# A decoder block's expert routing: logits taken from eight extra columns of the output product of the linear attention, ahead of the row norm

## The reference

```python
x = x + cross_attention(ln(x), ctx_1024)         # 16 heads, 1024 keys per batch and a null key
x = x + gated_linear_attention(ln(x))            # 4 heads; ends in o.reshape(b, n, 512) @ Wo
x = x + ffn(ln(x))
# ffn, with t = ln(x), 8 experts, top 2, at most 40 rows an expert:
scores = softmax(t @ wg)                         # wg: 256 x 8
gates, idx = top_k(scores, 2); gates /= sum(gates)
# rows go to their slots, y = fc2(silu(fc1(row) + b1)) + b2 per expert
res = t + sum(gates * y)
out = layernorm(res) * ln_gamma + ln_beta
```

## Time and profile before

| what | value |
| --- | --- |
| three timed runs, median | 213.72 us (212.79, 213.72, 213.93) |
| profiled execution, span from first to last instruction | 211.1 us |
| median less span | 2.6 us |
| TensorE busy | 193.9 us, 92% of the span |
| VectorE, ScalarE, GpSimd busy | 145.0, 118.1 and 39.0 us |
| mean granted TensorE clock | 0.988 |
| routing: from the first DVE instruction behind `lw_psum` to the first gather on TensorE | 162.85 to 168.99 us |
| experts: first `up` to last `combine` | 170.13 to 206.6 us |

### The profile page before, as it was taken

The page is one execution under the profiler, slowest core; times in us unless marked ns, Lnnn a source line. Parts: engine busy times, 40 slices in busy tenths (PEclk is TensorE's granted clock), DMA queues, the critical chain, the costliest instruction groups (busy, mean ns, idle before and its releaser), DMA issues.

```text
span 211.1 us, 4137 instructions
## 1 busy us (share of the span) xinstructions
PE 193.9 (92%) x1627; PEld 147.4 (70%) x1629; DVE 145.0 (69%) x249; ACT 118.1 (56%) x221; POOL 39.0 (18%) x40
## 2 busy tenths in 40 slices
PE   6796579999999999999999999999988899999991
PEld 1693469999889988899888787956655344645560
DVE  3449798989799799999979869633873727224313
ACT  3187678987779777797878764005631123332300
POOL 4129301304022040120400800020501400000001
PEclk9799999999999999999999999999999999999998
DMA  5896649693302003020000399999999400000000
GB/s 171 278 390 188 168 138 313 227 302 114 99 3 99 3 0 102 0 53 0 2 3 0 120 381 312 342 380 378 378 378 377 146 0 0 3 0 0 3 0 28
DMA packets 22853, 31.02 MB, mean 147 GB/s; under 512 B 1953, under 2 KB 18866, under 8 KB 22834
## 3 DMA queue, kind: packets, MB, share of 16 engines
q1 hardware_dynamic: 22834, 30.76, 43.6%
HBM read 29.57 MB, written 0.13 MB: 141 GB/s over the span
## 4 chain that ended last, share of the span: by engine, by line
PE 58%; issue 21%; DVE 9%; ACT 3%; DMA 3%; POOL 2%; SPq 1%; POOLq 0%; DVEq 0%; ACTq 0%
PE ps L1022 38%; PE ps L1056 7%; DMA w_k_stage<-in_Wkv 3%; DVE keys L745 3%; PE ps L1096 2%; PE ps L1110 2%; PE ps L1210 1%; PE ps L1010 1%; DVE q_split L736 1%; PE ps L1083 1%; DVE ex_l L711 1%; PE ps L1194 1%; PE ps L1249 1%; DVE ex_sum L766 1%; POOL hT L545 1%
## 5 line engine op out<-in xcount | busy, mean ns | idle before, releaser
L745 DVE SCALAR_TENSOR_TENSOR keys<-ps,keys 64x512 f16<-64x512 f32 x64 | 44.1, 689 | 2.3 <-ACT keys L577 0.3
L1022 PE MATMUL ps<-ctxT_h,w_k_h 128*128 128x256 f32 x128 | 38.1, 298 | 2.4 <-DVE keys L745 2.1
L577 ACT ACTIVATE keys<-ps 64x512 f16<-64x512 f32 x64 | 37.9, 592 | 1.8
L1022 PE MATMUL ps<-ctxT_h,w_k_l 128*128 128x256 f32 x128 | 36.6, 286 | 0.0
L1022 PE MATMUL ps<-ctxT_l,w_k_h 128*128 128x256 f32 x128 | 36.5, 285 | 0.0
L711 DVE TENSOR_TENSOR ex_l<-ps,ex_h 128x512 fp32r<-128x512 f32 x32 | 22.0, 689 | 11.1 <-ACT ps L607 11.0
L606 ACT ACTIVATE ex_h<-ps 128x512 fp32r<-128x512 f32 x32 | 19.1, 596 | 15.6 <-PE ps L1056 15.5
L1022 PEld LDWEIGHTS ps<-ctxT_h,w_k_h 128*128 128x128 f32 x128 | 24.8, 194 | 3.8 <-issue 3.0
L1022 PE MATMUL ps<-ex_h,ctx_h 128*128 128x512 f32 x64 | 25.4, 397 | 0.0
L1022 PE MATMUL ps<-ex_l,ctx_h 128*128 128x512 f32 x64 | 25.1, 392 | 0.0
L1022 PE MATMUL ps<-ex_h,ctx_l 128*128 128x512 f32 x64 | 24.9, 389 | 0.0
(11 more groups left out here) (175 smaller groups left out, 262.7 us busy)
## 6 DMA issues: line engine op xcount, KB each, us to landing
w<-in_fc1T SPq DMA_DIRECT2D x8, 1024.0 KB, 12.2
w<-in_fc SPq DMA_DIRECT2D x8, 1024.0 KB, 12.0
stage_t<-in_ctxT SPq DMA_DIRECT2D x8, 256.0 KB, 3.4
stage_n<-in_ctx SPq DMA_DIRECT2D x8, 256.0 KB, 2.7
w_k_stage<-in_Wkv SPq DMA_DIRECT2D x4, 256.0 KB, 6.5
mixT<-in_Wq SPq DMA_DIRECT2D x2, 512.0 KB, 6.2
q_two<-q_split SPq DMA_DIRECT2D x8, 128.0 KB, 4.0
w_v<-in_Wkv SPq DMA_DIRECT2D x1, 1024.0 KB, 6.8
```

The source lines that it names most:

```text
L577: nc.scalar.activation(keys[rows, u % 2, PK * i:PK * (i + 1), r], full[rows].rearrange("p (j n) -> p j n", j=PK), ACT.Copy, scale=UNIT).th ...
L745: V.scalar_tensor_tensor(out=keys[other, u % 2, PK * i:PK * (i + 1), r], in0=ps[mine, K_BANK + kp % 2].rearrange("p (j n) -> p j n", j=PK) ...
L1022: last = MM(dst, lhs[i], rhs[j], start=start and m == 0, stop=stop and m == len(parts) - 1)
```

## The change

The logits no longer wait for the normalised rows. Eight columns are added to the output product of the linear attention: `w_lo` becomes 264 wide, and its last eight columns are Wo times the router's weights with each of their columns centred (`w_rc`); `x1` becomes 264 wide too, its last eight columns being the centred logits of the layer's input, `xn` times `w_route` times the row's standard deviation. Bank 4 thus holds rows and centred logits together, the latter short of the factor 1/std of the row, which is applied only in the exponential (`scale=stat[:, 2, 9:10]`).

- SP loads Wo a second time, transposed on the host (`w_loT`, 512 KB), behind `w_lo`.
- TensorE: a product with ones for the column sums (in place of two of ten fillers), the eight-column product of `xn` behind the keys, eight products of `w_loT` with `w_rc` between L1231 and L1235, 264 instead of 256 columns in L1240 and L1249. The transpose of `xn`, the logit product and the seven fillers around them go; the `xn` product into bank 4 moves behind the first `up`. Three and eight fillers stand where six, one and six stood.
- DVE: `w_rc` (one instruction), the eight columns of `x1` (one), then after `lw_psum` the top-two search comes first and the statistics after it; it writes only the centred rows `xc`; `x2` moves between the two one-hots.
- ACT: a copy of 32 columns into `w_lo`; the copy of `xnT` goes; ACT writes `xn_h` and `xn` from `xc`.
- POOL: makes `xn_l` (before: DVE) and clears only the unused slots of `hT`.
- `share` takes the place of `ex_sum`'s memory, `silu` is halved in place, to make room.

```diff
-        x1 = keep("x1", [P, D])
+        x1 = keep("x1", [P, D + E])
...
-        w_lo = keep("w_lo", [P, LH, D])
+        w_lo = keep("w_lo", [P, LH, D + E])
+        w_loT = keep("w_loT", [P, DC, LH * LDV])
+        w_rc = keep("w_rc", [P, DC, E])
...
-        share = alloc(attn_b, "share", [P, G, PG, P])
+        share = ex_sum[:].rearrange("p h b s -> p (h b s)").rearrange("p (g x j t) -> p g x j t", g=G, x=2, j=PG)[:, :, 0]
...
+        fin = alloc(moe, "fin", [P, 2, D])
+        xc = fin[:, 0]
...
-            sp.dma_start(w_lo[:], chunked("lWo")).then_inc(ld_lin, 16)
+            sp.dma_start(w_lo[:, :, 0:D], chunked("lWo")).then_inc(ld_lin, 16)
+            sp.dma_start(w_loT[:], chunked("lWoT")).then_inc(ld_lin, 16)
...
-                    nc.gpsimd.memset(hT[:], 0.0).then_inc(zero_ready, 1)
+                    pool.wait_ge(xn_ready, 3)
+                    low_part(xn_l[:], xn[:], xn_h[:]).then_inc(xn_split, 1)
+                    nc.gpsimd.memset(hT[:].rearrange("p n c e s -> p (n c e) s")[:, :, CAP:SLOTS], 0.0).then_inc(zero_ready, 1)
...
+            act.wait_ge(w_lr_psum, 1)
+            copy(w_lo[:, :, D:D + E], ps[:, 0, 0:LH * E].rearrange("p (h e) -> p h e", e=E), w_lr_ready)
...
-            act.wait_ge(xnT_psum, 3)
-            copy(xnT[:], ps[:, 0, 0:DC * P].rearrange("p (c t) -> p c t", c=DC), xnT_ready)
+            act.wait_ge(xc_ready, 1)
+            act.wait_ge(rstd_ready, 3)
+            nc.scalar.activation(xn_h[:], xc, ACT.Copy, scale=stat[:, 2, 9:10]).then_inc(xnh_ready, 1)
+            act.wait_ge(xnh_ready, 1)
+            nc.scalar.activation(xn[:], xc, ACT.Copy, scale=stat[:, 2, 9:10]).then_inc(xn_ready, 1)
             act.wait_ge(below_ready, 1)
-            nc.scalar.activation(top_exp[:], below[:], ACT.Exp, accum_out=gate_sum[:, 0:1]).then_inc(top_exp_ready, 1)
+            nc.scalar.activation(top_exp[:], below[:], ACT.Exp, scale=stat[:, 2, 9:10],
+                                 accum_out=gate_sum[:, 0:1]).then_inc(top_exp_ready, 1)
...
+            dve.wait_ge(colsum_psum, 1)
+            V.scalar_tensor_tensor(out=w_rc[:], in0=ps[:, 4, 0:E].unsqueeze(1).broadcast_to([P, DC, E]), scalar=-1.0 / D,
+                                   in1=w_route[:], op0=ALU.mult, op1=ALU.add).then_inc(w_rc_ready, 1)
...
+            dve.wait_ge(x1_logit_psum, 1)
+            V.tensor_scalar(x1[:, D:D + E], ps[:, 0, 0:E], stat[:, 1, 8:9], stat[:, 1, 9:10], ALU.mult,
+                            ALU.mult).then_inc(x1_ready, 1)
...
-            norm_stats(2, ps[:, 4, 0:D])
-            normalise(2, xn[:], ps[:, 4, 0:D]).then_inc(xn_ready, 1)
-            V.tensor_tensor(x2[:], ps[:, 4, 0:D], beta[:], ALU.add).then_inc(x2_ready, 1)
-            dve.wait_ge(xn_ready, 3)
-            link(V.tensor_copy(xn_h[:], xn[:]))
-            low_part(xn_l[:], xn[:], xn_h[:]).then_inc(xn_split, 1)
-            dve.wait_ge(rl_psum, 1)
-            logits = ps[:, 1, 0:E]
+            logits = ps[:, 4, D:D + E]
             link(V.max(top[:], logits))
             link(V.max_index(top_idx[:], top[:], logits))
             V.tensor_tensor(pick[:], iota8.unsqueeze(1).broadcast_to([P, 2, E]),
                             top_idx[:, 0:2].unsqueeze(2).broadcast_to([P, 2, E]), ALU.is_equal).then_inc(pick_ready, 1)
+            norm_stats(2, ps[:, 4, 0:D])
+            V.tensor_scalar(xc, ps[:, 4, 0:D], stat[:, 2, 6:7], None, ALU.subtract).then_inc(xc_ready, 1)
             V.tensor_scalar(below[:], top[:], top[:, 0:1], None, ALU.subtract).then_inc(below_ready, 1)
...
             one_hot(slice(0, P))
+            V.tensor_tensor(x2[:], ps[:, 4, 0:D], beta[:], ALU.add).then_inc(x2_ready, 1)
             one_hot(slice(P, E * SLOTS))
...
-            warm(10, 7)
+            pe.wait_ge(ld_lin, 16 * 9)
+            pe.wait_ge(ld_const, 16)
+            for c in range(DC):
+                last = MM(ps[:, 4, 0:E], ones, w_route[:, c], start=c == 0, stop=c == DC - 1)
+            last.then_inc(colsum_psum, 1)
+            warm(8, 7)
...
+            for c in range(DC):
+                last = MM(ps[:, 0, 0:E], xnT[:, c], w_route[:, c], start=c == 0, stop=c == DC - 1)
+            last.then_inc(x1_logit_psum, 1)
...
+            pe.wait_ge(w_rc_ready, 1)
+            pe.wait_ge(att_ready, 1)
+            for h in range(LH):
+                for c in range(DC):
+                    last = MM(ps[:, 0, h * E:(h + 1) * E], w_loT[:, c, h * LDV:(h + 1) * LDV], w_rc[:, c], start=c == 0,
+                              stop=c == DC - 1)
+            last.then_inc(w_lr_psum, 1)
...
-            MM(ps[:, 4, 0:D], eye, x1[:], start=True, stop=False)
-            warm(6, 0)
+            pe.wait_ge(x1_ready, 2)
+            MM(ps[:, 4, 0:D + E], eye, x1[:], start=True, stop=False)
+            warm(6, 1)
...
-                last = MM(ps[:, 4, 0:D], loT[:, h], w_lo[:, h], start=False, stop=h == LH - 1)
+                if h == 0:
+                    pe.wait_ge(w_lr_ready, 1)
+                last = MM(ps[:, 4, 0:D + E], loT[:, h], w_lo[:, h], start=False, stop=h == LH - 1)
             last.then_inc(lw_psum, 1)
-            warm(6, 7)
-            transpose_xn(2)
-            warm(2, 7)
-            pe.wait_ge(xnT_ready, 3)
-            for c in range(DC):
-                last = MM(ps[:, 1, 0:E], xnT[:, c], w_route[:, c], start=c == 0, stop=c == DC - 1)
-            last.then_inc(rl_psum, 1)
-            pe.wait_ge(x2_ready, 1)
-            MM(ps[:, 4, 0:D], eye, xn[:], start=True, stop=False)
-            warm(1, 7)
+            warm(3, 7)
             pe.wait_ge(triangle_ready, 2)
             pe.wait_ge(pick_ready, 1)
             MM(ps[:, 2, 0:2 * E], strict_b[:], pick[:].rearrange("p k e -> p (k e)"), start=True, stop=False,
                skip_group_check=True)
             MM(ps[:, 2, E:2 * E], ones_b[:], pick[:, 0], start=False, stop=True, skip_group_check=True).then_inc(loc_psum, 1)
-            warm(6, 7)
+            warm(8, 7)
...
             up(0)
+            pe.wait_ge(x2_ready, 1)
+            MM(ps[:, 4, 0:D], eye, xn[:], start=True, stop=False)
...
+    arrays["lWoT"] = v["L0_attn_Wo"].T```

TensorE behind the last half of the output gate's product. Before (`decay_p` is `loT`, `qx` under L1244 is the gated heads):

```order
L1231 MATMUL ps<-w_lg,xnT 128x512
L1235 MATMUL ps<-lv,att 128x128 x4
L1240 MATMUL ps<-x,const 128x256
L1010 MATMUL ps<-warmer 128x512 x6
L1244 MATMUL ps<-const,qx 128x128 x4
L1249 MATMUL ps<-w_lo,decay_p 128x256 x4
```

More of the change, by code:

```diff
@@ L650, in _ @@
             act.wait_ge(g_psum, 1)
-            nc.scalar.activation(silu[:, 0], ps[:, 5], ACT.Tanh, scale=0.5).then_inc(gtanh_ready, 1)
+            nc.scalar.activation(silu[:], ps[:, 5], ACT.Tanh, scale=0.5).then_inc(gtanh_ready, 1)
+            act.wait_ge(w_lr_psum, 1)
+            copy(w_lo[:, :, D:D + E], ps[:, 0, 0:LH * E].rearrange("p (h e) -> p h e", e=E), w_lr_ready)
             for h in range(LH):
@@ L1368 @@
     arrays["ctxT"] = arrays["ctx"].T
+    arrays["lWoT"] = v["L0_attn_Wo"].T
     arrays["Wgk2b"] = np.concatenate([v["L0_attn_Wgk2"], v["L0_attn_bgk2"][None, :]])
```

21 lines of the change are left out of this document (12 added, 9 removed).

## The result

| | before | after |
| --- | --- | --- |
| median of 19 runs each | 213.57 us | 212.28 us |
| lowest to highest run | 211.77 to 215.06 | 210.91 to 213.32 |
| ratio, with its 95% interval | | 0.9951 (0.9931 to 0.9971) |
| span of the profiled execution | 211.1 us | 211.2 us |

By the ratio the kernel is faster by 1.05 us (0.6 to 1.5); the two medians by themselves differ by 1.29, which lies in that interval. The forecast was 0.88 us less and 212.8 us, made against a median of 213.72.

What follows compares the result with a forecast made beforehand. TensorE was taken to bound from the first `up`, a serial routing path before it. -2.09 + 0.71 + 0.05 + 0.45 = -0.88 us, from 213.72 to 212.8 us; range 212.0 to 214.1.

Steps and rivals of the forecast that it cites:

- The bound: From the first `up` on TensorE bounds; bringing the first gather forward comes off the end, work added to TensorE goes on.
- Term 1: Routing path from T (first DVE instruction behind `lw_psum`) to the first gather's load: 6.14 us becomes 4.05, gain 2.09.
- I hold `below` until the power ends.: Routing on DVE: `below` waits for POOL's power on the shared memory port, until T+2.04; escaping would gain 0.13 us more.
- the rival of the longer rows' branch: Power, two ACT passes, POOL: passes up to half longer than 0.417 us, gather moves 0.43, result 213.3 us; chance 0.08.
- The collision, "T+4.05": One-hot's second half and POOL's `xn_l` meet on the shared port near T+3.0; gather at T+4.05 instead of undisturbed T+3.85.
- Term 2: Eight products of `w_loT` and `w_rc` before the values: 16 instructions at 0.11 us, 0.71 us lost.
- the rival that ended slower: The eight weight products do not pipeline, each fresh load shows: 214.1 or 215.2 us; chance 0.04.
- Term 3: Eight more columns in the output product (L1249): 0.05 us lost.
- Term 4: The `xn` product moved behind the first `up`, where TensorE has no gap: 0.45 us lost.
- T at 163.6: Expected profile sign: the first DVE instruction behind `lw_psum`, at 162.85 before, comes at 163.6 us.
- At nothing: Column sums, `w_rc`, `x1` logits, SP's extra load, shortened clearing and `x2` between the one-hots: covered by waits, no cost.
- The clock: Rival: 1.5 us idle before the gather halves TensorE's clock at the first `up`, costing 1.35 us, 214.2 us; chance 0.08.

Runs made afterwards that it cites:

- Run 8: Changed kernel plus a 256-column DVE copy ahead of `below`, under POOL's power; one run, no ratio, gather 4.04 us after the first DVE instruction behind `lw_psum`.
- run 7: Changed kernel with `x2` written before the first one-hot; one run, no ratio, gather 4.07 us after the first DVE instruction behind `lw_psum`.
- Run 6: Changed kernel with `xn_l` made on DVE behind the first one-hot and POOL's clearing of `hT` held back; ratio to the kernel before 0.9934.
- Runs 3: Changed kernel with statistics and `xc` ahead of the search on DVE, fillers 8 and 5 instead of 3 and 8; ratio to the kernel before 0.9982.
- 5: Changed kernel with statistics and `xc` ahead of the search, and POOL's clearing of `hT` held until both one-hots are written; ratio to the kernel before 0.9935.
- run 1: Changed kernel with the `xn` product in place of two fillers between first gather and first `up`; ratio to the kernel before 0.9919.
- run 9: Changed kernel without the three fillers ahead of the counts and the eight behind them; ratio to the kernel before 1.0057.

## Why the prediction was right, step by step

**The bound.** Right. What the experts' stage got earlier came off the end: from the second `up` to the last norm's second instruction of statistics (207.08 us before, 207.22 after) it is 31.58 or 31.59 us in all twelve profiles, so nothing ahead of the second `up` was given back behind it. In nine kernels the three distances up to there give the measured ratio within its interval.

**Term 1, 6.14 to 4.05: the size was right (4.03), the mechanism was not.** The start held: power from T+1.49 to T+2.04, to the hundredth, and the statistics at T+0.58. Three steps behind it failed.

- *"I hold `below` until the power ends."* It was not held. It ran under the power (T+1.72 to T+1.94), `place` started at T+1.85 instead of T+2.08, the one-hot at T+2.43 instead of T+2.67, and its second half was through at T+3.10, before POOL began. Run 8 shows the same for a copy of 256 columns. The Trainium skill, "SBUF — State Buffer", section "Who interferes with whom", says that such copies between SBUF tensors and GpSimd block each other for the whole instruction. It agrees with `xn_l` and the clearing here (0.73, 1.40, 1.51 us) and not with a power of one element per partition, 0.55 us long. Nor did show both directions in full: POOL's subtractions, with 0.58 us of L736 still to run, grew by only 0.21 (3.13 less four times 0.73), as in run 7, where 0.17 was left and 0.04 was added.
- *"xn_h and xn, each like the exponential of 256 columns, 0.417."* With a per-row scale each pass took 0.51. This is the rival of the longer rows' branch, at half its size: instead of T+2.93 the passes ended at T+3.18, and `xn_l` at T+3.97. The Trainium skill, "ScalarE: Activation LUTs", section "What ACT_TABLE_LOAD costs", states that an operand with one value per partition adds about 93 ns to an activation; this trace agrees, 0.51 against 0.417. The two differ in function too (a copy and an exponential); the exponential of 8 columns, which got the same scale by the change, went from 0.21 to 0.28 us.
- *The collision, "T+4.05".* There was none on the path. The undisturbed rows' branch was forecast to release the gather at T+3.85; it did so at T+4.03, through 0.19 us more in ACT's passes and 0.06 more in front of them, less 0.07 behind (`xn_l` 0.72, the gather 0.06 after it instead of 0.11). I had put 0.20 on the collision instead. Run 6 shows that this branch alone set the gather. Two errors of nearly the same size and opposite sign met, so that 4.03 came out is luck; the expected sign in the profile, a longer L952 or `xn_l`, was absent (0.35 and 0.72), and by that the working was wrong at the right total.

The collision itself is real, a step later: the 384-column L951 took 1.51 us, over `xn_l` and the clearing, under cover of the first gather and `up`. Runs 3 and 5 brought it onto the path and priced it: an instruction of 0.29 took 0.73 over one POOL instruction and 1.40 over two. The kernel before had it as well, which the prediction did not read:

```profile
165.13 1.07 DVE L909 CAST xn_h<-xn 128x256 fp32r<-128x256 f32 x1
```

It ran until 166.20, 0.14 past the end of POOL's clearing. That hold is no part of the gain worth naming: the logits' product ends at 166.46 by the profile, and the search started at 166.58.

**Term 2, 0.71 lost: 0.65 to 0.66.** The sixteen starts lie 0.106 us apart, not 0.11. The products pipeline, so the rival that ended slower had nothing for it.

**Term 3, 0.05 lost.** 0.71 between the gate's half and T, less 0.65, leaves 0.06; the output product itself shows 2.05 us instead of 1.99.

**Term 4, 0.45 lost: 0.42,** and run 1 shows that the whole was to be had back.

**T at 163.6.** 164.68 less the 1.12 us by which this execution was late is 163.56.

**At nothing.** The edits ahead of the gate's second half (column sums, `w_rc`, the logits in `x1`) cost nothing: from the second norm's first statistics to that half it is 15.94 us before (138.31 to 154.25) and after (139.43 to 155.37). SP's queue waits for `ctx_l` as it did (50.9 us in five waits, against 52.3 in six of the earlier trace rows). SP's load of `w_loT` starts at 44.22 us, behind the point (39.41) from which the two executions keep their distance up to the second norm. The edits behind the search (`xn_h` and `xn` on ACT, `xn_l` on POOL, the early search) lie in the distances above. Apart from runs 3 and 6 they were not tried each alone, so how the 2.11 us of term 1 divide among them is not shown.

**The clock.** It stayed at 1.00 with 1.29 us without work ahead of the gather, and fell with 3.03 (run 9), to a loss of 1.54. The rival's price of 1.35 was near; its condition was not met. At the start of the program, where the prediction says that TensorE had been busy for less than half of the time, it was busy for 2.07 us from 4 to 8 us.

**Chances.** The measured 0.9951 lies on the line between "faster by over 0.5%" and "within 0.5%", which were given 0.40 and 0.52. The sum of -0.88 was 0.10 short of the -0.98 by distances: 0.02 in term 1, 0.05 in terms 2 and 3, 0.03 in term 4.

## What to carry to other kernels

A step that moves off the critical path changes which branch ends last; write down the end of each branch with its own instructions' durations (here 0.51 for the ACT form used, not 0.417 for its neighbour) before pricing a collision between them. Filler work is a list of free places: a real product belongs where a filler stands (0.44 us each time here), and the fillers that then remain may still be what keeps the clock. And keep an engine that shares a port from starting its unurgent work (a clearing) right behind its urgent one, while the other engine waits to issue (1.40 us instead of 0.73 here).

## What the runs showed of the hardware that was not expected

- POOL's power of one element per partition lasts 0.55 us and leaves DVE free: a DVE instruction of 0.22 and a copy of 256 columns in 0.28 us ran entirely under it. A 256-column subtraction on POOL holds a DVE instruction that issues 0.08 behind it to 0.73 us.
- A held DVE instruction can be passed over by POOL's next one when that follows at once (1.40 us for 128 columns, which take 0.29 alone, and 1.51 for 384), and can also get in between (0.88, with POOL's clearing at 0.95 instead of 0.74). What decides stays open.
- An ACT pass of 256 columns from SBUF takes 0.51 us with a scale per row and 0.417 without.
- Matmuls of 8 columns with a fresh 128 x 128 float32 load each follow one another at 0.106 us, sixteen in a row.
- The low stretch of TensorE's clock in the first 30 us lies at different places in different executions (8 to 11 us in one, 22 to 26 in another), and the second of these came out 1.12 us later behind it. Runs 1 and 3 have no low stretch there and still reach the second norm at 137.62 and 138.93 us; they differ by 1.26 us already at 22.5 to 23.7 us, and why stays open. Either is as large as the effect studied, so spans of two single executions can't be set against each other.
